# Both ends of an eight-part decoder kernel put in another order, with one core

## What is computed

```
x = x + L0_xattn(ln(x), ctx)     # 16 heads of 8, softmax over 64 keys
x = x + L0_ffn(ln(x))            # 8 routed SwiGLU experts (top 2) and 2 shared ones
x = x + L1_xattn(ln(x), ctx)     # attention between channels
x = x + L1_ffn(ln(x))            # 8-bit quantised linear layer
x = x + L2_xattn(ctx, ln(x))     # deformable attention, 5 sampled points per head
x = x + L2_ffn(ln(x))            # 8 experts with GELU for the first 512 rows
x = x + L3_xattn(ln(x), ctx)     # 16 heads with bias, mask, clamps of nan and inf
x = x + L3_ffn(ln(x))            # gated, with fake quantisation of every stage
```

## Time and profile before

| | |
|---|---|
| median of 3 runs | 476.1 us |
| the three runs | 476.1, 476.27, 471.72 us |
| profiled execution | 471.51 us |
| its span, first to last instruction | 469.7 us |
| mean granted TensorE clock | 0.967 |
| TensorE busy / VectorE busy / ScalarE busy | 84% / 77% / 53% |

### The profile page before, as it was taken

How to read it: one execution, slowest core, us unless ns; L and a number is a source line. 1 busy time by engine, 2 the same in 40 slices (tenths; PEclk the granted TensorE clock), 3 DMA queues, 4 the chain that set the end, 5 groups by cost and what they waited for, 6 DMA issues and landing times.

```text
span 469.7 us, 8627 instructions
## 1 busy us (share of the span) xinstructions
PE 393.7 (84%) x3391; PEld 259.2 (55%) x3391; DVE 363.0 (77%) x805; ACT 247.9 (53%) x429; POOL 110.7 (24%) x95
## 2 busy tenths in 40 slices
PE   4999889999999988786887888899999995678056
PEld 1656556566666667553454446575667763553045
DVE  3799656648544587889878898999898789777985
ACT  3764853324223334457787884855866334435931
POOL 3200000005990001006995345210410133000000
PEclk9999999999999999989999999999999998979659
DMA  7880000000000000026000003000000000000001
GB/s 241 354 298 3 2 1 0 2 0 1 0 1 0 1 3 2 0 98 262 2 1 0 3 1 68 1 1 2 0 1 1 2 0 1 3 0 0 1 0 46
DMA packets 11084, 16.51 MB, mean 35 GB/s; under 512 B 5274, under 2 KB 9764, under 8 KB 10148
## 3 DMA queue, kind: packets, MB, share of 16 engines
q1 hardware_dynamic: 10756, 15.17, 9.2%
q10 hardware_dynamic: 288, 0.79, 0.5%
HBM read 15.43 MB, written 0.52 MB: 34 GB/s over the span
## 4 chain that ended last, share of the span: by engine, by line
PE 48%; DVE 32%; ACT 11%; issue 6%; DMA 1%; POOL 1%; DVEq 0%; ACTq 0%
PE ps L808 7%; PE ps L813 7%; PE ps L847 7%; PE ps L2075 4%; PE ps L241 3%; DVE arena L613 2%; PE ps L2065 2%; DVE arena L616 2%; DVE arena L1862 2%; PE ps L1714 2%; DVE stats L251 2%; PE ps L2102 1%; DVE arena L635 1%; DMA ctx_fm<-in_ctx_fm 1%; PE ps L2617 1%
## 5 line engine op out<-in xcount | busy, mean ns | idle before, releaser
L926 DVE SCALAR_TENSOR_TENSOR arena<-ps,cols,arena 128x512 f32<-128x512 f32 x40 | 29.8, 750 | 42.3 <-PE ps L813 38.0
L822 ACT ACTIVATE arena<-ps,cols 128x512 f32<-128x512 f32 x40 | 27.4, 687 | 63.9 <-PE ps L808 63.9
L241 PE MATMUL ps<-const 128*128 128x256 f32 x152 | 40.1, 412 | 7.4 <-ACT arena L2658 4.4
L847 PEld LDWEIGHTS ps<-weights,arena 128*128 128x128 f32 x320 | 38.5, 192 | 8.1 <-issue 8.0
L1862 DVE TENSOR_SCALAR arena<-ps 128x512 f32<-128x512 f32 x56 | 36.4, 684 | 7.3 <-PE ps L1700 3.5
L847 PE MATMUL ps<-weights,arena 128*128 128x128 f32 x320 | 39.2, 276 | 0.2 <-DVE x_tm L915 0.2
L241 PEld LDWEIGHTS ps<-const 128*128 128x128 f32 x152 | 29.8, 205 | 16.4 <-ACT arena L2658 4.7
L813 PE MATMUL ps<-h_fm,weights 128*128 128x512 f32 x80 | 37.7, 593 | 0.7 <-DVE arena L926 0.7
L808 PE MATMUL ps<-h_fm,weights 128*128 128x512 f32 x80 | 37.7, 594 | 0.6 <-ACT h_fm L382 0.6
L2065 PE MATMUL ps<-h_fm,weights 128*128 128x512 f32 x64 | 30.3, 606 | 2.7 <-ACT arena L2443 1.8
L1700 PE MATMUL ps<-l2buf,picks_b 128*128 128x256 bf16 x160 | 25.5, 275 | 6.5 <-DVE arena L1862 4.7
(11 more groups left out here) (391 smaller groups left out, 880.5 us busy)
## 6 DMA issues: line engine op xcount, KB each, us to landing
weights<-in_moe_w SPq DMA_DIRECT2D x2, 2048.0 KB, 9.9
weights<-in_moe_w SPq DMA_DIRECT2D x3, 1280.0 KB
l2buf<-in_picks SPq DMA_DIRECT2D x1, 1664.0 KB, 7.9
rows<-in_rows SPq DMA_DIRECT2D x1, 1024.0 KB, 13.1
x_tm<-in_x SPq DMA_DIRECT2D x2, 256.0 KB, 5.0
ctx_fm<-in_ctx_fm ACTq DMA_DIRECT2D x1, 512.0 KB, 5.7
ctx_tm<-in_ctx SPq DMA_DIRECT2D x1, 512.0 KB, 14.0
mats<-in_mats SPq DMA_DIRECT2D x1, 512.0 KB, 14.4
```

Source lines behind the costliest of these rows:

```text
L241: PE.matmul(ps[:, bank, 0:256], ident, const[:, 0:256], start=True, stop=True)
L822: AC.activation(silu[:, k, :], ps[:, k, :], ACT.Silu, bias=bias_col(0, e, k)).then_inc(silu_ok, 1)
L847: ins = PE.matmul(ps[:, 4 + u % 2, P * t:P * t + P], glu[:, u % 2, k, P * t:P * t + P], w3[:, e, k, :], start=(k == 0), stop=(k == 1))
L926: V.scalar_tensor_tensor(out=glu[:, u % 2, k, :], in0=ps[:, 2 + k, :], scalar=bias_col(1, e, k), in1=silu[:, k, :], op0=ALU.add, op1=ALU.m ...
```

## The change

- Front: seven products on a memset tile ahead of the K products. The first norm is done in halves. Queries of the first half and scores of tile 0 go ahead of the second half's queries and of value groups 1 to 3. The second half of the spread keys moves from VectorE to ScalarE, into steps 1 and 2 of the loop; the value spread moves behind the first exponential.
- Deformable stage: the table load for the exponential goes ahead of `keep_queries(1)`; the three broadcast banks are taken in another order, so that the first broadcast doesn't wait for the query tile; `move(2)` and its copy go ahead of `sample(1)` and `other_side`; the key operations move from ahead of step 0 into steps 1 (one) and 3 (two).
- Last expert: tiles 0 to 2 are summed in banks 0 to 2, and only tile 3 waits. Identity products: 4 to 2 ahead of the late rows, new ones (2, 4, 2, 2) in the last attention.
- Last attention: `project(1)`, `project(2)` earlier on TensorE; VectorE's last part and ScalarE's copies and exponentials in another order.
- `ffn3`: half of the input rounding on ScalarE; the up maxima spread between the gate roundings; chunk 1's product on GpSimd; ten identity products become eight; the output is rounded in pieces of 128, 256, 128 and 512 tokens, the second and the last begun by ScalarE.

The diff, cut to its core:

```diff
@@ first clear, and the seven products ahead of the K products
+            pool_link(G.memset(arena[:, 0:384], 1.0))
             G.memset(v4[:], 0.0).then_inc(cleared, 1)
...
+                pe.wait_ge(pool_chain, 1)
+                for _ in range(7):
+                    PE.matmul(ps[:, 0, 0:256], arena[:, 0:P], arena[:, P:P + 256], start=True, stop=True)
                 pe.wait_ge(mats0_in, 16)
@@ attention(), TensorE, ScalarE and VectorE of the first layer
                 scores(0)
-                stay_busy(pe, 2, 6)
+                l0_norm.wait_turned(pe)
+                l0_queries(pe, 1)
+                l0_values(pe, 1)
+                l0_values(pe, 2)
+                l0_values(pe, 3)
...
                     if t == 0:
-                        stay_busy(pe, 3, 6)
+                        stay_busy(pe, 2, 6)
...
+                    if t == 0:
+                        spread_l0_values(act, (0, 1))
+                        spread_l0_values(act, (2, 3))
...
+                    if t in (1, 2):
+                        spread_l0_keys(act, (2 * t - 2, 2 * t - 1))
...
+                    if t == 0:
+                        for g in range(1, 4):
+                            keep_l0_values(dve, g)
@@ first_keys_values(): layernorm(between=keep_keys) and the blocks behind it give way to
+            def spread_late_keys(act, heads):
+
+                src = k_fm[:, 512:1024].rearrange("p (b k) -> p b k", b=8)
+                act.wait_ge(k_sb, 2)
+                for h in heads:
+                    ins = AC.activation(kx[:, 8:16, h], src, ACT.Copy, scale=const[:, C_HM + h:C_HM + h + 1])
+                if heads[-1] == 3:
+                    ins.then_inc(kx_ready, 1)
...
+            @block.tensor
+            def _(pe):
+                pe.wait_ge(const_in, 16)
+                first.turn(pe, 4)
+                values(pe, 0)
+                first.wait_turned(pe)
+                queries(pe, 0)
+                second.turn(pe, 5)
...
+                act.wait_ge(cleared, TABLE_SET)
+                first.root(act)
+                first.apply_on_act(act, (2, 3))
+                act.wait_ge(cols_in, 16)
+                keep_keys(0)
+                second.root(act)
+                keep_keys(1)
+                first.keep_turned(act, 4)
+                second.apply_on_act(act, (2, 3))
+                act.wait_ge(bq_ok, 1)
+                keep_queries(act, 0)
+                second.keep_turned(act, 5)
+                AC.activation(table[:, 1:2], table[:, 0:1], ACT.Exp)
+                keep_queries(act, 1)
@@ deformable(): table load, banks, order
                 second_norm.keep_turned(act, 4)
+                AC.activation(warm, const[:, C_BIAS1:C_BIAS1 + 1], ACT.Exp)
                 keep_queries(1)
...
-                        ins = PE.matmul(ps[:, m % 3, 256 * i:256 * i + 256], picks_b[:, 2 * c + i, :],
+                        ins = PE.matmul(ps[:, (m + 2) % 3, 256 * i:256 * i + 256], picks_b[:, 2 * c + i, :],
...
-                    if c < 2:
-                        pe.wait_ge(qt_ok, c + 1)
-                    if c == 2:
+                    if c == 0:
                         pe.wait_ge(off_sb, 4)
+                    if c in (1, 2):
+                        pe.wait_ge(qt_ok, c)
...
+                    if w == 1:
+                        move(pe, 2)
                     if 0 < w < NW:
                         sample(w)
-                    if w == 1:
-                        move(pe, 2)
...
-                AC.activation(warm, const[:, C_BIAS1:C_BIAS1 + 1], ACT.Exp)
...
+                    if w == 1:
+                        keep_positions(act, 2)
                     for c in mine:
                         other_side(w // 2 + 1, c)
-                    if w == 1:
-                        keep_positions(act, 2)
...
-                bound_last_keys(dve)
...
+                    if w == 1:
+                        find_last_keys(dve)
+                    if w == 3:
+                        bound_last_keys(dve)
@@ experts_and_last_attention()
-            SUM_BANK, LAST_BANKS = 3, (3, 0, 1, 2)
+            SUM_BANK, LAST_BANKS = 3, (0, 1, 2, 3)
...
-                    if e >= 1:
-                        pe.wait_ge(sum_added, e)
                     for j in range(4):
+                        if e >= 1 and (j == 3 if e == NE - 1 else j == 0):
+                            pe.wait_ge(sum_added, e)
...
-                stay_busy(pe, 4, 2)
+                stay_busy(pe, 2, 2)
                 late_rows.turn(pe, 0)
...
                 turn(4, 1)
+                stay_busy(pe, 2, O_BANKS[4])
                 weigh_values(4)
+                pe.wait_ge(of_ready, 4)
+                stay_busy(pe, 4, O_BANKS[7])
                 turn(5, 0)
                 turn(5, 1)
+                stay_busy(pe, 2, O_BANKS[5])
                 weigh_values(5)
                 project(0)
                 turn(6, 0)
                 turn(6, 1)
+                stay_busy(pe, 2, O_BANKS[6])
                 weigh_values(6)
+                project(1)
                 turn(7, 0)
                 turn(7, 1)
+                project(2)
                 weigh_values(7)
-                project(1)
-                project(2)
                 project(3)
...
-                logits(7)
+                weigh_scores(7)
+                clear_nan(6)
+                maximum(7)
                 less_last_max()
-                clear_nan(6)
+                divide(5)
+                clear_nan(7)
+                divide(6)
                 add(0)
-                clear_nan(7)
-                divide(5)
                 add_stats(0)
-                divide(6)
                 add(1)
                 add_stats(1)
                 divide(7)
...
+                for t in range(LATE - 1, NT):
+                    exponential(t)
+                    keep_turned(t, 0)
+                    keep_turned(t, 1)
@@ ffn3()
-                stay_busy(pe, 10, 5)
+                stay_busy(pe, 8, 5)
...
+                AC.activation(h_fm[:, 512:1024], h_fm[:, 512:1024], ACT.Identity, bias=magic, scale=inv[:, X:X + 1])\
+                    .then_inc(gm_ok, 1)
...
+                maxima(1, range(1))
                 gate_round(0)
+                maxima(1, range(1, 2))
                 gate_round(1)
-                maxima(1, range(2))
...
-                weigh_gate(0)
-                weigh_gate(1)
-                ins = weigh_gate(2)
-                dve_link(ins)
+                bounded = bound_share(0)
+                shares_bounded.append(bound_share(1))
+                product = weigh_gate(0, bounded)
+                all_max(dve, UP)
+                dve.wait_ge(dve_chain, product)
+                gate_maximum(0)
+                bounded = bound_share(2)
+                product = weigh_gate(2, bounded)
+                dve.wait_ge(dve_chain, product)
+                gate_maximum(2)
+                dve.wait_ge(gate1_ok, 1)
+                dve_link(gate_maximum(1))
...
+                first, last = tokens(up, 0, 128), tokens(up, 384, 128)
...
+                pool.wait_ge(g_ok, 2)
+                pool.wait_ge(dve_chain, shares_bounded[0])
+                G.tensor_tensor(chunk(gate, 1), chunk(gate, 1), chunk(sig, 1), ALU.mult).then_inc(gate1_ok, 1)

```

191 lines of the change are left out of this document (93 added, 98 removed).

## The result

The changed kernel took 467.34 us (median of 464.2, 466.01, 468.66 and 469.21), against 474.92 for the kernel before beside it (471.72 to 476.27): ratio 0.9845, 95% interval [0.9802, 0.9888]. Forecast was 466.8 us against a median of 476.1. The profiled execution took 464.2 us with a span of 462.4, so 7.3 less than the profiled one of before, where the terms of the forecast add up to 9.3.

What follows compares the result with a forecast made beforehand. No engine bounds the kernel (chain: TensorE 48%, VectorE 32%, ScalarE 11%). Terms -1.9 - 0.6 - 1.5 - 2.0 - 3.3 = -9.3 from the median 476.1 give 466.8; own range 461.5 to 469.5, with some rivals 460.5 to 471.5.

Steps and rivals of the forecast that it cites:

- Front, -1.9 forecast: Front: tile 4 starts at 29.6 instead of 31.51; ends 0 if K products stay slow, -3.3 if key spreads aren't last.
- Deformable, -0.6 forecast: Deformable stage: earlier table load wins 0.75, key operations at step 3 give back up to 0.9; -0.6, ends 0 and -1.2.
- Rival D: Deformable stage: the table load costs its drain as well, +1.3, giving 468.1; chance 0.04.
- Guard, -1.5 forecast: Experts to last attention: free banks and two fewer identities start the query guard at 375.0, not 376.52; ends -0.9 and -1.9.
- Tail, -2.0 forecast: Last attention's end: VectorE's idle of 2.31 goes, about 0.3 comes back; -2.0, ends -0.5 and -2.5.
- Last feed-forward, -3.3 forecast: Last feed-forward: input rounding, gate scale, fewer identities and smaller first output piece together win 3.3.
- (a): Last feed-forward: half of the input rounding on ScalarE spares waiting for the second of two operations; -0.35.
- (b): Last feed-forward: chunk 1's product on GpSimd and shares bounded early; -2.05, net -1.75 after GpSimd's contention.
- (c): Last feed-forward: ten identity products become eight ahead of the output maximum, ending near 455.8; -0.85.
- (d): Last feed-forward: first output piece of 128 tokens, not 256, starts the 48 products earlier; -0.35 of 1.48 idle.
- E: TensorE stays at its lower clock where identity products were cut; slower by 2.0, 478.1; chance 0.04.
- F: Whole kernel: the change does little, moved waits are replaced nearly one for one; 473 to 477, chance 0.05.

Runs made afterwards that it cites:

- old banks: Changed kernel with the last expert's sums back in their old banks and the ten identity products added in the last attention left out: 465.93 us.
- old tail: Changed kernel with TensorE's and VectorE's old order at the last attention's end and one identity product instead of three at ffn3's start: 472.49 us.
- ScalarE's old order: Changed kernel with ScalarE's loop of exponentials and copies in the last attention as in the kernel before, nothing else: 465.64 us.
- changed kernel again: The changed kernel unchanged, run once more on the same chip as its improved version: 465.70 us, ratio 0.9801 to the kernel before.
- filled gap: Changed kernel with four identity products in TensorE's front wait, the table load at its old place and ffn3's input rounded by VectorE: 464.19 us.
- better kernel: Changed kernel with late key spreads on GpSimd and TensorE kept busy by identity products in moe0 and through the last feed-forward: 460.15 us, ratio 0.9691.

## Why the prediction was right, and where it wasn't

The time was right (466.8 forecast, 467.3 measured), the side and the range too. That it came to within 0.5 is luck: I took 9.3 off a median of 476.1, which lies at 474.92 with the fourth run, and the medians differ by 7.6. In the profiles the sum was 2.0 too large; the terms were off by more, in both directions, and partly cancel.

**Front, -1.9 forecast, -0.46 measured.** The steps were right: K products, tile 0, tile 4, the late keys as the last thing waited for. What failed is the step, taken without a reason, that this wait costs only itself. A wait of TensorE opened the way for a fall of the clock, and the fall took 1.33 of 1.79; filling the wait gives them back, taking it away gives 2.56, so -3.0, near my end of -3.3. The link is the firmest of those on the clock: with the wait of some 2.2 all seven profiles have a fall near 30 (in three, those of the old banks, the old tail and ScalarE's old order, it lasts 6.83 and costs 2.8), without it none of five has one. The bound at the other end was too mild: cold, the kernel's front would have been 1.9 behind the old one. **Between the stages, 0 forecast, +1.63 measured**: the fall in `moe0`. It is not an effect of the change's code there. In eight profiles of the new order without an edit at that place it is there and costs 1.6 in six, and is away in two (the changed kernel again, the filled gap); with two narrow products in the pause ahead of it, it is there in none of four. The pause of 0.72 can't be the whole cause: the kernel before and the two profiles without the fall have it too. Nor is its absence all gain. Of the six profiles of the new order without this fall, five have one between 206 and 221 that costs 1.5 or more (all but the better kernel's); of the six with it, two do. What decides where a fall comes stays open.

**Deformable, -0.6 forecast, -1.81 measured.** Mis-sized twice. `move(2)` ahead of the sampling gave 1.07, where I had 0.9 and then took it back: the two key operations at step 3 were to overrun their idle by 0.9, and they took 1.57 instead of the 2.2 that I had from the earlier trace rows, and delayed nothing. GpSimd worked beside them both times: before it was a two-input operation and a cast, here it is a one-input operation, which itself took 1.59 where it otherwise took 1.07. The table load's place gave some 1.0 rather than 0.75, the key operations nothing by themselves, and 0.25 to 0.84 hang on which softmax operations meet GpSimd's. The 1.07 and the 1.0 add up to more than the 1.81, so the second is too high or the two overlap; no run separates that. Rival D is refuted: the query copy follows the load by 1.40. By the Trainium skill, "ScalarE: Activation LUTs", What ACT_TABLE_LOAD costs, it would have followed by 2.66; the trace decides against it.

**Guard, -1.5 forecast, -1.84 measured.** Banks 1.15 and identities the remaining 0.69, where I had 0.9 and 0.6. **Tail, -2.0 forecast, -2.72 measured**, at my outer end of -2.5 and past it. The step that ScalarE's new order costs and gives nothing was wrong: it is worth 1.60 of the 2.72, and only beside VectorE's new order; the added identities (ten; I had counted eight) gave 0.21, as good as the nothing that I forecast. Of VectorE's and TensorE's order no clean price is on record, since the run without it has a fall in it.

**Last feed-forward, -3.3 forecast, -2.12 measured.** (a) -0.35 became +0.36. The step missed TensorE's identities, which end at 415.6 at half clock whatever rounds the input; at full clock the part is worth 0.21 to 0.28. (b) -1.75 became -1.97, of which GpSimd's product is worth 0.88 and the rest lies with the shares bounded early and the new order. The product took 3.20 and not the 2.5 of my estimate, and it cost nothing, since its maximum follows chunk 2's, near 439; the share operation stretched by 0.24. The Trainium skill, "GPSIMD Engine Reference", Key points, names as colliding those VectorE operations that have two SBUF inputs or run in a two-port mode. The rows agree for the softmax operations (0.32 alone, 0.87 beside GpSimd) and not for VectorE's own product, which kept its 1.22; the share operation has one input, and no row shows its mode. (c) -0.85 became -0.24: ten identities less two were 6.32 less 0.25, because five and a half of the eight run at half clock, where four of the ten did. (d) about -0.3, as forecast.

**The rivals.** E had the right engine and the wrong place: not the number of identities at the end, but pauses earlier. Its mechanism (the clock fails to rise) is refuted with four of them. F's view, waits replaced one for one, holds for (a) and (c) only.

## What to carry over

When an edit moves the wait onto TensorE, price what runs behind it at half clock as well, and put identity products into the wait; they cost nothing while they end in time, and they hold up a maximum when they themselves run at half clock. A new order of several engines is one edit: ScalarE's alone taken back cost 1.6, the other two's under ScalarE's new one 5.0 (with a fall of the clock in it), where all three had won 2.7. Read parts by the shift of the same instruction in two profiles; totals of single executions of the changed kernel differ by 5 us, and the mean clock with them (0.963 to 0.956).

## What the hardware did that I had not expected

- The same program has its stretches of half clock in other places from run to run: 30.5, 95.4 and 201.2, or 29.4, 206.9 and 213.7. One costs 0 (from 201), 1.3 or 2.8 (front), 1.6 (`moe0`), 1.5 each (start of the deformable stage) or 1.9 (from 219 and 221), by what the chain runs on there. The Trainium skill, "TensorE: Matmul & The Clock Gate", Part 1, says of a kernel's first products that the same kernel shows different counts of slow ones from run to run; the traces show the like in the middle of a kernel. The forecast should have carried a term for it: the changed kernel again lost 4.4 us by such falls (1.3 in the front and 3.05 ahead of the first hat), the kernel with the old tail 7.4 (2.8, 1.6 and 3.0).
- GpSimd: four 128 x 512 products with a scalar took 6.92 us, one two-input product of 128 x 1024 took 3.20 beside VectorE's and 1.90 to 2.75 elsewhere (VectorE: 1.67 and 1.22). VectorE's small two-input operations took 0.87 and 0.83 beside GpSimd's, 0.32 and 0.44 alone.
- Ahead of the trace's first clock record the clock column reads 1.00 although products take twice their time; there the duration has to be read.
